# A graph-network kernel: the ratio of the label counts is computed from the PSUM bank of the counts

## The reference

```python
mask = (adj[None] == labels[:, None, None, None])            # labels 1..4
weight = mask / (jnp.sum(mask, axis=-1, keepdims=True) + EPS)
agg = jnp.einsum('dbmn,bnh->bmdh', weight, hid).reshape(B, N, D * H)
out = relu(agg @ Wd.T + bd)
r = sigmoid(out @ Wri.T + bri + hid @ Wrh.T + brh)
z = sigmoid(out @ Wzi.T + bzi + hid @ Wzh.T + bzh)
n = tanh(out @ Wni.T + bni + r * (hid @ Wnh.T + bnh))
out = (1.0 - z) * n + z * hid
return layernorm(out) * gamma + beta
```

## Time and profile before

| | |
|---|---|
| median of 3 runs | 566.2 us (565.68 to 566.47) |
| profiled execution, its own time | 565.02 us |
| its span in the trace | 563.2 us |
| mean granted clock of PE | 0.991 of full speed |
| PE busy | 518.4 us, 92% |
| DVE busy | 466.9 us, 83% |
| ACT busy | 412.2 us, 73% |
| POOL busy | 365.6 us, 65% |
| ratio, line 1487 | 42.3 us in 28 instructions |

### The profile page before, as it was taken

The page is one execution under the profiler, slowest core; times in us unless marked ns, Lnnn a source line. Parts: engine busy times, 40 slices in busy tenths (PEclk is TensorE's granted clock), DMA queues, the critical chain, the costliest instruction groups (busy, mean ns, idle before and its releaser), DMA issues.

```text
span 563.2 us, 10546 instructions
## 1 busy us (share of the span) xinstructions
PE 518.4 (92%) x2951; PEld 438.6 (78%) x2951; DVE 466.9 (83%) x1077; ACT 412.2 (73%) x791; POOL 365.6 (65%) x368
## 2 busy tenths in 40 slices
PE   7987889999999999999999999999999999999993
PEld 4776777887787878788788778788788788878892
DVE  5897758888889888888988888888888898888887
ACT  5837777787787787677777778778778777777872
POOL 2967566676776676676676676667667667666435
PEclk9998999999999999999999999999999999999997
DMA  8111022111122111112211112111112210211111
GB/s 305 60 46 48 29 76 67 43 51 51 54 67 65 61 32 65 37 65 65 65 31 62 44 58 65 65 50 43 64 39 65 65 65 28 65 37 38 38 40 56
DMA packets 20261, 33.42 MB, mean 59 GB/s; under 512 B 2256, under 2 KB 6992, under 8 KB 20240
## 3 DMA queue, kind: packets, MB, share of 16 engines
q1 hardware_dynamic: 19872, 32.38, 17.5%
q10 hardware_dynamic: 288, 0.52, 0.3%
q0 software_dynamic: 80, 0.26, 0.1%
HBM read 24.77 MB, written 8.39 MB: 59 GB/s over the span
## 4 chain that ended last, share of the span: by engine, by line
DVE 40%; PE 27%; issue 15%; ACT 7%; POOL 7%; DMA 1%; DVEq 1%; ACTq 0%; POOLq 0%
PE alpha L410 11%; PE p_bank L447 6%; PE gamma L410 5%; PE y_bank L410 5%; DVE ratio L1487 4%; DVE shared L1497 4%; DVE mix L1508 4%; DVE masks L1177 4%; DVE shared L1513 3%; DVE y_lo L1490 3%; ACT shared L1042 3%; DVE mix L1462 3%; ACT shared L1047 2%; DVE out_rows L1449 2%; DVE out_rows L1446 2%
## 5 line engine op out<-in xcount | busy, mean ns | idle before, releaser
L447 PE MATMUL p_bank<-y_hi,masks 128*128 128x256 f32 x256 | 75.4, 316 | 16.2 <-POOL y_lo L1874 9.8
L995 ACT ACTIVATE p_bank<-p_bank,ratio 128x256 f32<-128x256 f32 x112 | 45.5, 444 | 55.7 <-PE p_bank L447 55.7
L1860 POOL TENSOR_TENSOR shared<-x_rows,shared 128x512 f32<-128x512 f32 x28 | 35.9, 1284 | 65.3 <-ACT shared L1042 65.3
L447 PEld LDWEIGHTS p_bank<-y_hi,masks 128*128 128x128 f32 x256 | 48.3, 189 | 38.1 <-DVE out_rows L1449 16.4
L447 PE MATMUL p_bank<-y_lo,masks 128*128 128x256 f32 x256 | 66.6, 282 | 0.0
L1852 POOL TENSOR_TENSOR x_lo<-x_f,x_hi 128x1024 fp32r<-128x1024 f32 x27 | 64.9, 2402 | 1.2 <-ACT x_hi L1008 1.2
L410 PE MATMUL alpha<-wx_hi,x_hi 128*128 128x384 f32 x122 | 47.2, 387 | 13.4 <-ACT shared L1047 12.0
L1843 POOL TENSOR_TENSOR var_eps<-mean_var,ln_eps 128x2 f32<-128x2 f32 x27 | 5.3, 197 | 82.2 <-DVE mean_var L1473 82.2
L410 PEld LDWEIGHTS alpha<-wx_hi,x_hi 128*128 128x128 f32 x122 | 22.9, 188 | 38.3 <-ACT shared L1047 23.9
L447 PEld LDWEIGHTS p_bank<-y_lo,masks 128*128 128x128 f32 x256 | 48.7, 190 | 0.1
L1446 DVE SCALAR_TENSOR_TENSOR out_rows<-p_bank,rcount,bd_rows 128x256 f32<-128x256 f32 x56 | 25.7, 458 | 26.6 <-PE p_bank L447 26.6
(11 more groups left out here) (311 smaller groups left out, 1866.6 us busy)
## 6 DMA issues: line engine op xcount, KB each, us to landing
x_f<-in_xT SPq DMA_DIRECT2D x32, 256.0 KB, 2.6
x_rows<-in_x SPq DMA_DIRECT2D x32, 256.0 KB, 2.6
out<-shared SPq DMA_DIRECT2D x31, 256.0 KB, 2.0
adj_in<-in_adjT SPq DMA_DIRECT2D x32, 128.0 KB, 2.0
shared<-in_wgT SPq DMA_DIRECT2D x2, 576.0 KB, 6.2
shared<-in_wdT ACTq DMA_DIRECT2D x2, 256.0 KB, 5.2
vec_rows<-in_vectors SPq DMA_DIRECT2D x1, 512.0 KB, 6.4
shared<-in_wgT SPq DMA_DIRECT2D x2, 192.0 KB, 6.9
```

The source lines that it names most:

```text
L447: last = nc.tensor.matmul(p_bank[:, b * H:(b + 1) * H], masks[:, k % 2, g, d, :], part[:, g, d * H:(d + 1) * H], start=first, stop=(part i ...
L995: nc.scalar.activation(p_bank[:, b * H:(b + 1) * H], p_bank[:, b * H:(b + 1) * H], ACT.Copy, scale=ratio[:, k % 2, g, b:b + 1]).then_inc(p ...
L1860: nc.gpsimd.tensor_tensor(from_n[:, :], x_rows[:, m % 2, :, :].rearrange("p g f -> p (g f)"), n_sb[:, :], ALU.subtract).then_inc(from_read ...
```

## The change

The ratio is made by one `scalar_tensor_tensor` that reads the raw counts from `t_bank` (PSUM), adds EPS and multiplies by `rcount`, in place of a `tensor_tensor` that reads `rcount` and `counts`, both in SBUF. The copy `counts` stays, since the reciprocal reads it. Because `t_bank` is now read later, PE's wait ahead of the transposes is for `ratio_ready` instead of `counts_ready`. The order of the instructions is the same on all engines. Only `fast_step` is changed; the steps before it keep the old form.

```diff
@@ PE, fast_step
                 pe.wait_ge(out_ready, up(2 * i, 2))
-                pe.wait_ge(counts_ready, up(i + 1))
+                pe.wait_ge(ratio_ready, up(i + 1))
                 transposes()
@@ DVE, fast_step
                 sum_labels(i - 1, 1)
                 dve.wait_ge(rcount_ready, up(i + 1))
-                nc.vector.tensor_tensor(ratio[:, i % 2, :, :], rcount[:, i % 2, :, 0:4:2],
-                                        counts[:, i % 2, :, 1:4:2], ALU.mult).then_inc(ratio_ready, 1)
+
+                nc.vector.scalar_tensor_tensor(ratio[:, i % 2, :, :],
+                                               t_bank[:, 0:2 * D].rearrange("p (g d) -> p g d", g=2)[:, :, 1:4:2], EPS,
+                                               rcount[:, i % 2, :, 0:4:2], ALU.add, ALU.mult).then_inc(ratio_ready, 1)
```

## The result

| | before | after |
|---|---|---|
| median of 4 runs | 566.22 us (565.68 to 566.47) | 552.4 us (551.1 to 553.05) |
| profiled execution, own time | 565.02 us | 552.9 us |
| its span | 563.2 us | 551.1 us |
| mean granted clock of PE | 0.991 | 0.992 |

The ratio of the times is 0.9754, 95% interval 0.9733 to 0.9775, so the change took away 2.5%. The forecast was 552.4 us.

The account below looks back on a forecast made before the run. It took the chain from DVE's held ratio through `tanh` and POOL to PE's products as the bound. 20 x 0.55 + 6 x 0.46 = 13.8 us off 566.2 us gave 552.4 us, range 548.0 to 560.0.

Parts of the forecast that it names:

- The ratio is held by POOL's `x_lo` because it reads two SBUF tiles: DVE's ratio: held to the end of `x_lo`; with one input in PSUM it takes 0.16 us, ending at 291.82, not 293.30.
- Most of the 1.48 us is lost again at `y_lo`, which waits for ACT: DVE's line 1490: waits for ACT's line 1026, starts at 292.57 instead of 293.22, so only 0.65 us is left.
- 1508 is still held, by 1737, and goes in ahead of 1741: DVE's line 1508: ends 0.55 us after POOL's 1737, at 295.06, gaining 0.55 us; 0.46 us in six steps.
- The gain goes on unchanged to PE: From 1508 over `tanh` to PE: nothing else gives; PE's wait for line 1047 falls from 23.9 to 10 to 14 us.
- The transposes don't wait: PE ahead of the transposes: hears of the ratio at 292.06, reaches them at 292.39; cost nothing, cover 0.33 us.
- 26 steps, 13.8 us: Sum over the steps: 20 x 0.55 + 6 x 0.46 = 13.8 us; the two short instances gain nothing.
- 1741 goes first: Rival at DVE's line 1508: POOL's 1741 gets in ahead, 1508 ends at 295.61 as now; 566.2 us, 10%.
- 1508 isn't held: Rival at DVE's line 1508: it ends at 294.85, a gain of 0.76 us; 548.2 us, 8%.
- The slower case: Rival at PE's transposes: ratio still held by POOL, 0 to 0.26 us per step more, middle 3.4 us; 569.6 us, 5%.
- The half gain: Rival beside the chain: something takes over half-way, gain 6.9 us; 559.3 us, 13%.
- The estimate of 0.065 us more for a PSUM source: New ratio by the skill's table, 120 against 58 fixed cycles: 26 times, 1.7 us if unhidden; 554.1 us.

Follow-up runs that it names:

- the table of four: Ratio by `tensor_tensor` or `scalar_tensor_tensor`: from two SBUF tiles 566.2 and 566.0 us, with one input in PSUM 552.57 (EPS left out) and 552.4 us.
- the held reordering: Kernel before, ratio still from two SBUF tiles, with the two normalisation instructions put ahead of `y_lo` but behind the ratio: 566.74 us, ratio 1.0015.

## Why the prediction was right, point by point

- *The ratio is held by POOL's `x_lo` because it reads two SBUF tiles.* Shown by the table of four. The size was 0.152 us where I took 0.16 us.
- *Most of the 1.48 us is lost again at `y_lo`, which waits for ACT.* 24.6 us of idle time ahead of it; it starts 0.88 us after the start of the ratio, and I had 0.91 us. That is 0.68 us earlier than before, forecast 0.65 us.
- *1508 is still held, by 1737, and goes in ahead of 1741.* Its end came 0.56 us behind the end of 1739 (1737 before), and 1743 (1741) was stretched to 0.79 us, as in the earlier trace rows. The gain at this point, counted from the start of the ratio, is 3.95 us before and 3.40 us after, 0.55 us. This was the step on which most hung: with 1508 unheld the time would have been 548.2 us.
- *The gain goes on unchanged to PE.* `tanh` starts 0.76 us behind the end of 1510, as before. PE's wait for 1047 in this step is 0.56 us, the total 14.4 us, just above the 10 to 14 us that I gave: the wait is 0.33 us shorter than before, not 0.55 us, since PE's product ahead of it starts earlier as well. The prediction follows the gain only over `tanh`. The way over `y_lo` and line 1035, which the held reordering laid open, was shortened by the change too: PE's wait for 1035 fell from 12.1 to 8.0 us.
- *The transposes don't wait.* Right, and with more room than I gave it: the hand-over from DVE to PE is 0.06 us, and 0.93 us of waiting there cost nothing.
- *26 steps, 13.8 us.* The medians differ by 13.8 us. In the profiled executions 13.1 us lie between the first and the last ratio, and 12.1 us in the whole span; the steps are mostly 16.18 us apart, where I had 16.15 us. That the medians meet the forecast to 0.1 us is in part luck: the four runs of the kernel before spread over 0.8 us, those of the kernel after over 2.0 us.
- *The rivals.* That 1741 goes first, and that 1508 isn't held, are refuted by the rows above. The slower case was priced too high: its term of 0.13 us per step, the middle of 0 to 0.26 us, came out at zero when it was run alone. The half gain didn't show. The estimate of 0.065 us more for a PSUM source would not have reached the time either: 0.21 us more per step at this place cost nothing.

One thing agrees with the Trainium skill (SBUF — State Buffer, section "SBUF: two separate sides"), which states that a VectorE instruction with two SBUF inputs and a GpSimd instruction that reads SBUF exclude each other on shared ports for a whole instruction. The table of four and the 1.25 us of line 1508 above agree with it; the ports themselves no run here shows. Another doesn't show here. From the Trainium skill's table of 120 fixed cycles for a PSUM source and 58 for an SBUF source (VectorE: DVE Perf Modes, section "The TRN2 errata — SBUF-src ops pay a fixed extra latency per instruction") the prediction estimated 0.065 us more. The pair in this case measured 0.152 us from PSUM and 0.151 us, the shortest, from SBUF. The measurement decides; at four elements the durations show no such price.

## What to carry to other kernels

A tiny instruction with a long duration and no idle time ahead of it is being held; look at what the other engines do at the moment at which it ends. When it is freed, follow the queue to the next instruction of the same kind and to the next wait, since the gain is what is left after those (0.55 of 1.48 us here). Follow every way out of the held queue, not only the one that ends last: here `y_lo` fed PE by a way of its own. Then fill the wait that opened: moving two independent instructions into it brought another 11 us. The same move with the hold still there brought nothing, since it made `y_lo` late.

## What the runs showed of the hardware

- In the steps read here, a DVE instruction with two inputs in SBUF ran only beside an idle POOL or between POOL's instructions. One that arrived 0.05 us after the start of a 0.74 us POOL instruction took 1.25 us instead of 0.69 us. Between two POOL instructions queued 0.08 us apart DVE got its turn, and the second one was stretched from 0.46 to 0.79 us.
- With one input in PSUM the ratio ran beside POOL's 2.4 us `x_lo` in 0.149 to 0.154 us, for both kinds of instruction.
- Four of these small DVE instructions in a row, without waits between them, start 0.07 us apart though each is shown with 0.15 us, so that three more of them took 0.21 us of the queue, where I had expected 0.3 to 0.45 us.
